# Order of loads, memsets, q and k of chunk 1, quad 0's loads and the last scores in a fused mixer, FFN and attention kernel

## What is computed

```python
x = x + _L0_attn_a_ref(_layernorm(x, axis=-1), ...)   # sigmoid gate, conv of 4 and of 9 taps, linear maps
x = x + _L0_ffn_ref(_layernorm(x, axis=-1), ...)      # relu(h)**2 between two ternary matrices
x = x + _L0_attn_b_ref(_layernorm(x, axis=-1), ...)   # q, k, v; softmax(q k / sqrt(8)) v; out_w
x = x + _L0_ffn_ref(_layernorm(x, axis=-1), ...)
```

## Time and profile before

| | us |
|---|---|
| median of three runs (548.97 to 550.91) | 549.75 |
| the profiled execution's own time | 550.75 |
| its span in the trace | 548.8 |
| TensorE matmuls busy | 508.4 (93%) |
| VectorE busy | 448.9 (82%) |
| ScalarE busy | 355.5 (65%) |
| GpSimd busy | 63.4 (12%) |

### The profile page before, as it was taken

How to read it: one execution, slowest core, us unless ns; L and a number is a source line. 1 busy time by engine, 2 the same in 40 slices (tenths; PEclk the granted TensorE clock), 3 DMA queues, 4 the chain that set the end, 5 groups by cost and what they waited for, 6 DMA issues and landing times.

```text
span 548.8 us, 10459 instructions
## 1 busy us (share of the span) xinstructions
PE 508.4 (93%) x4214; PEld 234.3 (43%) x4214; DVE 448.9 (82%) x666; ACT 355.5 (65%) x680; POOL 63.4 (12%) x89
## 2 busy tenths in 40 slices
PE   1999997997598999999999999999999999999797
PEld 1455455675233333333333333333333333343476
DVE  5799149977698899999999999999999999711853
ACT  2646322433003788888888888888888888887431
POOL 4690002841000000000000000000000000000000
PEclk9999999899655899999999999999999999999999
DMA  8100000023710030201200200200200000000001
GB/s 216 26 3 2 1 1 1 4 81 120 227 37 1 2 79 23 57 2 26 55 3 22 59 3 19 61 2 20 61 2 2 2 2 3 1 2 1 1 20 58
DMA packets 14074, 17.97 MB, mean 33 GB/s; under 512 B 3599, under 2 KB 10174, under 8 KB 13502
## 3 DMA queue, kind: packets, MB, share of 16 engines
q1 hardware_dynamic: 13000, 16.58, 11.1%
q0 software_dynamic: 240, 0.46, 0.4%
q10 hardware_dynamic: 786, 0.27, 0.2%
HBM read 11.70 MB, written 5.24 MB: 31 GB/s over the span
## 4 chain that ended last, share of the span: by engine, by line
PE 81%; DVE 10%; ACT 3%; SPq 2%; issue 1%; DMA 1%; ACTq 1%
PE ps L1235 30%; PE ps L1283 26%; PE ps L1006 7%; PE ps L1016 5%; DVE mx L920 4%; PE ps L1250 4%; PE ps L1027 2%; DVE h L705 2%; PE ps L1052 1%; PE ps L1038 1%; PE ps L1063 1%; DVE x L813 1%; DVE st L682 1%; ACT gate L651 1%; SPq L338 1%
## 5 line engine op out<-in xcount | busy, mean ns | idle before, releaser
L920 DVE TENSOR_REDUCE mx<-ps 128x1 f32<-128x1024 f32 x256 | 311.4, 1224 | 18.7 <-PE ps L1235 16.6
L1235 PE MATMUL ps<-kt,qt 62*128 62x512 f32 x512 | 198.2, 473 | 8.9 <-DVE mx L920 4.6
L1250 PE MATMUL ps<-qt,kt 64*128 64x512 f32 x512 | 188.6, 448 | 1.0 <-ACT gate L651 1.0
L651 ACT ACTIVATE acc<-ps 128x512 f32<-128x512 f32 x256 | 139.2, 597 | 27.4 <-PE ps L1250 22.0
L651 ACT ACTIVATE gate<-ps 128x512 f32<-128x512 f32 x256 | 138.7, 597 | 16.3 <-PE ps L1250 10.4
L1235 PEld LDWEIGHTS ps<-kt,qt 62*128 62x128 f32 x512 | 82.1, 198 | 114.5 <-DVE mx L920 86.0
L1283 PE MATMUL ps<-gate,val 128*32 128x256 f32 x1024 | 82.7, 395 | 3.8 <-ACT gate L651 3.8
L1250 PEld LDWEIGHTS ps<-qt,kt 64*128 64x128 f32 x512 | 77.7, 186 | 11.7 <-ACT gate L651 5.4
L1283 PE MATMUL ps<-acc,val 128*32 128x256 f32 x1024 | 81.6, 391 | 0.4 <-ACT acc L651 0.4
L1283 PEld LDWEIGHTS ps<-gate,val 128*32 128x32 f32 x1024 | 20.2, 108 | 49.3 <-issue 26.8
L1283 PEld LDWEIGHTS ps<-acc,val 128*32 128x32 f32 x1024 | 20.2, 108 | 46.7 <-ACT acc L651 23.4
(11 more groups left out here) (180 smaller groups left out, 389.0 us busy)
## 6 DMA issues: line engine op xcount, KB each, us to landing
kt<-k_scr SPq DMA_DIRECT2D x32, 128.0 KB
qt<-q_scr SPq DMA_DIRECT2D x64, 64.0 KB
x<-in_L_attn_a_x SPq DMA_DIRECT2D x4, 256.0 KB, 5.2
q_scr<-attn SPq DMA_DIRECT2D x4, 256.0 KB, 2.6
k_scr<-attn SPq DMA_DIRECT2D x4, 256.0 KB, 3.1
q_scr<-gate SPq DMA_DIRECT2D x4, 256.0 KB, 2.7
k_scr<-gate SPq DMA_DIRECT2D x4, 256.0 KB, 2.7
qt<-nm_s SPq DMA_DIRECT2D x64, 4.0 KB
```

What stands on the lines that cost most here:

```text
L651: act.activation(pexp[step % NPB][:, j, :], bank(e_bank(slot)), ACT.Exp, scale=SCALE).then_inc(e_read, 1)
L920: dve.tensor_reduce(mx[:, item % 2, at:at + 1], pair(lo), AX.X, ALU.max).then_inc(m_read, 1)
L1235: mm = pe.matmul(bank(m_banks(M_UNIT[u])[keys]), qt[r][rows, half, jj, c * P:(c + 1) * P], kt[r][rows, jj, keys, :], start=True, stop=True)
L1250: pe.matmul(bank(e_bank(slot)), kt[r][rows, jj, s // TC, s % TC * P:(s % TC + 1) * P], qt[r][rows, half, jj, :], start=True, stop=True).th ...
```

## The change

Nothing is computed differently. What moves:

- **Loads.** SP issues x parts 0 and 1, then hb_w, ha_w and fuse_w (512 KB, new semaphore `s_w_fold`), then x parts 2 and 3; taps, the other mixer weights and the FFN's small ones follow, and the two big ternary inputs come last.
- **Roots and folded weights.** ScalarE takes `first_std(0)` as its first work and `first_std(1)` only after the four values of batch 0. TensorE turns hb_w, ha_w and fuse_w right behind in_w, and the vectors (`vec_n`) after the first two `turn_h` and no longer ahead of them.
- **Zeroing.** GpSimd's memsets of `qt`, `kt` and `v4` no longer wait for the mixer's last tokens but for the end of the convolutions (`conv_done`) and for `u_mm`; the row of ones comes from `fu_n`; the bias on x is added between quads of the attention.
- **q and k of chunk 1.** `turn_h`, `qk` and `v` of chunk 1 come ahead of `proj(2)`; VectorE does `qkv_out(0)` and `qkv_out(1)` together; ScalarE copies chunk 2 before its root.
- **Quad 0 in parts.** q of the first query half is loaded as soon as chunk 0 is stored, k after chunk 1, q of the second half last, on a semaphore of its own (`q1_in`) for which only the second item waits.
- **The last 12 steps.** Heads go in the order 2, 0, 3, 1, `pv` is one part of 512 columns, and from the second of these steps banks 4 and 5 join the three banks of the scores.

```diff
+LAST_HEAD = 1
+LATE_HEADS = (2, 0, 3, 1)
+LATE_EBANKS = (4, 5)
+def has_units(hn, s):
+    return HT * (hn + 1) + LEAD + 2 * s < NU
+def heads(hn, s):
+    return HEADS if has_units(hn, s) else LATE_HEADS
...
 def e_bank(slot):
-    return EBANKS[slot % len(EBANKS)]
+    if slot < E_LATE:
+        return EBANKS[slot % len(EBANKS)]
+    at = (slot - E_LATE) % (len(EBANKS) + len(LATE_EBANKS))
+    return EBANKS[(E_LATE + at) % len(EBANKS)] if at < len(EBANKS) else LATE_EBANKS[at - len(EBANKS)]
...
-            for c in range(NCH):
+            def load_x(c):
                 sp.dma_start(x[:, TC * c:TC * c + TC, :], x_src[:, TC * c:TC * c + TC, :]).then_inc(s_x[c], 16)
+            load_x(0)
+            load_x(1)
+            for dst, src in ((hb_n[:, :], hb_w), (ha_n[:, :], ha_w),
+                             (fu_n[:, :, :], fuse_w.rearrange("(k p) c -> p k c", p=P))):
+                sp.dma_start(dst, src).then_inc(s_w_fold, 16)
+            load_x(2)
+            load_x(3)
...
-            for i in range(2):
-                sp.wait_ge(scr_done[i], STORED)
-            load_quad(0)
+            sp.wait_ge(scr_done[0], STORED)
+            load_q(0, 0)
+            sp.wait_ge(scr_done[1], STORED)
+            load_k(0)
+            load_q(0, 1)
...
-            pool.wait_ge(tok_read, TOK_MIX[-1] + 1)
+            pool.wait_ge(setup_mm, 4)
+            pool.memset(ones_home, 1.0).then_inc(consts_ready, 1)
+            pool.wait_ge(conv_done, 2 * B)
+            for r in range(NBUF):
+                pool.memset(qt[r][:, :, :, :].bitcast(F32), 0.0).then_inc(consts_ready, 1)
+                pool.memset(kt[r][:, :, :, :].bitcast(F32), 0.0).then_inc(consts_ready, 1)
+            pool.wait_ge(u_mm, 1)
...
+            first_std(0)
             act.wait_ge(s_norm, 16)
             ev(1, flat(in_T), bank(1), ACT.Identity, scale=norm_col[:, 0:1])
-            first_std(0)
...
-                if c >= 2:
-                    qkv_out(c - 2)
+                if c == 2:
+                    qkv_out(0)
+                    qkv_out(1)
                 take_tokens(TOK_F1, c)
...
+            turn_h(2, TURN_QKV + 1)
             qk(0)
             v(0)
-            turn_h(2, TURN_QKV + 1)
-            proj(2, 0, TOK_F1)
             qk(1)
             v(1)
+            proj(2, 0, TOK_F1)
             proj(3, 0, TOK_F1)
...
+                    if not has_units(hn, s):
+                        for j in LATE_HEADS:
+                            exp_mm(hn, s, j)
+                        pv(step - 1, 0, CH)
+                        continue
```

More of the change, by code:

```diff
@@ L87, in plan @@
                 turned_o[hn // 2 - 1] = next(m)
-            for j in HEADS:
+            for j in heads(hn, s):
                 exps[hn, s, j] = next(e)
@@ L277, in build @@
         qk_in = [sem(f"qk_in{r}") for r in range(NBUF)]
+        q1_in = [sem(f"q1_in{r}") for r in range(NBUF)]
         shift_in, v4_ready = sem("shift_in"), sem("v4_ready")
@@ L304, in _ @@
                 sp.dma_start(dst, src).then_inc(s_w_taps, 16)
-            sp.dma_start(wfc_n[:, :, :], wfc_d.rearrange("(m p) d -> p m d", p=P)).then_inc(s_w_tern, 16)
-            sp.dma_start(wpr_n[:, :], wproj_d).then_inc(s_w_tern, 16)
-            for dst, src in ((pw_n[:, :, :], pw_w.rearrange("(k p) c -> p k c", p=P)), (hb_n[:, :], hb_w),
-                             (ha_n[:, :], ha_w), (fu_n[:, :, :], fuse_w.rearrange("(k p) c -> p k c", p=P)),
-                             (ow_n[:, :], out_w), (bm_n[:, :], Bm_d)):
+            for dst, src in ((ow_n[:, :], out_w), (bm_n[:, :], Bm_d),
+                             (pw_n[:, :, :], pw_w.rearrange("(k p) c -> p k c", p=P))):
                 sp.dma_start(dst, src).then_inc(s_w_mix, 16)
@@ L334, in load_quad, with load_q @@
                         sp.dma_start(dst.rearrange("x j h t -> x (j h t)"), src).then_inc(qk_in[n % NBUF], 16)
-                        for half in range(2):
-                            src = q_scr[i, b, half, rows, :, :].rearrange("d j t -> d (j t)")
-                            dst = qt[n % NBUF][at:at + PARTS * HD, half, :, :].bitcast(F32)
-                            sp.dma_start(dst.rearrange("x j t -> x (j t)"),
-                                         src.unsqueeze(1).broadcast_to([HD, PARTS, RJ * CH])).then_inc(
-                                             qk_in[n % NBUF], 16)
+            def load_q(n, half):
+                b, g = divmod(n, GQ)
+                landed = (qk_in, q1_in)[half][n % NBUF]
+                for a in range(2):
+                    rows = slice((a * GQ + g) * HD, (a * GQ + g + 1) * HD)
+                    for i in range(PARTS):
+                        at = a * HALF + i * PARTS * HD
+                        src = q_scr[i, b, half, rows, :, :].rearrange("d j t -> d (j t)")
+                        dst = qt[n % NBUF][at:at + PARTS * HD, half, :, :].bitcast(F32)
+                        sp.dma_start(dst.rearrange("x j t -> x (j t)"),
+                                     src.unsqueeze(1).broadcast_to([HD, PARTS, RJ * CH])).then_inc(landed, 16)
+            def load_quad(n):
+                load_k(n)
+                load_q(n, 0)
+                load_q(n, 1)
             def load_shift(hn):
@@ L423, in _ @@
             pool.wait_ge(v4_zero, NV)
-            for r in range(NBUF):
-                pool.memset(qt[r][:, :, :, :].bitcast(F32), 0.0).then_inc(consts_ready, 1)
-                pool.memset(kt[r][:, :, :, :].bitcast(F32), 0.0).then_inc(consts_ready, 1)
-            pool.memset(ones_rows, 1.0).then_inc(consts_ready, 1)
             for r in range(NV):
@@ L430, in _, with bias_rows @@
             pool.wait_ge(v4_ones, NV)
-            for c in range(NCH):
+            def bias_rows(c):
                 tiles = slice(TC * c, TC * (c + 1))
@@ L647, in _ @@
                         act.wait_ge(pv_mm, step - NPB + 1)
-                    for at, j in enumerate(HEADS):
+                    for at, j in enumerate(heads(hn, s)):
                         slot = E_EXP[hn, s, j]
@@ L1268, in turn_o, with pv @@
                 mm.then_inc(m_mm, 1)
-            def pv(step, part):
+            def pv(step, lo_q, hi_q):
                 hn, s = divmod(step, BT)
                 n, half = divmod(hn, 2)
-                if part == 0:
-                    pe.wait_ge(e_read, E_EXP[hn, s, HEADS[-1]] + 1)
+                if lo_q == 0:
+                    pe.wait_ge(e_read, E_EXP[hn, s, LAST_HEAD] + 1)
                 first, last = (half, s) == (0, 0), (half, s) == (1, BT - 1)
-                if first and part == 0:
+                if first and lo_q == 0:
                     pe.wait_ge(v4_ready, n + 1)
@@ L1280, in pv @@
                         pe.wait_ge(o_copied, n)
-                lo, cols = VPAD * (1 - half), slice(part * CH // 2, (part + 1) * CH // 2)
+                lo, cols = VPAD * (1 - half), slice(lo_q, hi_q)
                 for j in range(QH):
                     mm = pe.matmul(bank(O_BANK)[VW * j:VW * (j + 1), cols], v4[n % NV][:, s, j, lo:lo + VW],
-                                   pexp[step % NPB][:, j, cols], start=first and part == 0, stop=last and part == 1,
+                                   pexp[step % NPB][:, j, cols], start=first and lo_q == 0, stop=last and hi_q == CH,
                                    tile_position=(0, VW * j))
-                if part:
+                if hi_q == CH:
                     mm.then_inc(pv_mm, 1)
```

125 lines of the change are left out of this document (73 added, 52 removed).

## The result

The changed kernel takes 534.75 us (median of four runs, 534.02 to 536.34), beside 549.92 us for four runs of the kernel before (548.97 to 550.91): a ratio of 0.973, 95% interval 0.970 to 0.976, some 15 us. The prediction was 536.2 with a range of 531.5 to 541. The profiled execution of the changed kernel took 534.02 us with a span of 532.0, so span against span it is 16.8 us shorter; it was the shortest of its four.

The account below looks back on a forecast made before the run. TensorE was taken as the bound most of the time, with five places to gain. Terms of -0.2 + 0.9 + 3.3 + 4.0 + 5.5 = 13.5 us off 550.75 gave 537.2, as a median 536.2, range 531.5 to 541.

Parts of the forecast that it names:

- start: From launch to the first products: x part 2 lands later and takes back other savings, a loss of 0.2 us.
- folded weights: Eight transposes move from TensorE's full stretch at 43.62 into a rest before the first h: gain of 0.9 us.
- zeroing: FFN 1: without memsets beside them four tensor_scalar run faster and TensorE's clock stays at 2.4 GHz: gain of 3.3 us.
- q and k of chunk 1 with quad 0 in parts: Way into attention: first scores wait for the last v at 138.6, not loads at 142.65: gain of 4.0 us.
- last steps: Last 12 attention steps: eleven fall from 2.46 to ScalarE's pace of 1.96 us: gain of 5.5 us.
- the units and first exponentials: At the first scores: the clock was taken to fall to half again, so no gain.
- the ternary part would be stretched to about 14 us: VectorE's ternary weights beside the moved memsets: tensor_scalar held up by them, lasting to about 70.3, costed at nothing.
- rival 2: Last steps: pv and scores hand over too late, step stays near 2.26; gain 2.2 there, 539.5 us; chance 0.15.
- estimate of 4.2: Last steps: the skill's exponential price of 0.52 us gives a step of 2.08 and this smaller gain; the row was preferred.
- rival 3: First scores: the clock stays at 2.4 GHz when the units follow at once; 2.4 us more, 533.8; chance 0.15.
- Rival 5: Last steps: the clock falls and stays low to the end; 559.2 us as a median, at least; chance 0.02.
- Rival 4: FFN 1: the clock falls anyway or gating slips past 77.7; price 1.7 to 2.6 us, 538.3; chance 0.13.

Follow-up runs that it names:

- zero_old: The changed kernel with the zeroing of qt, kt and v4 back behind the mixer's last tokens; 538.31 us.
- folds_late_x_first: folds_late with all four parts of x ahead of the three folded weights on the load queue; 535.82 us.
- seven kernels with the changed start: The changed kernel and six follow-up kernels whose start was not edited; they reach the first transpose of ow_n at 40.47 to 42.16 us.
- folds_late: The changed kernel with the eight transposes of hb_w, ha_w and fuse_w back behind the taps; 538.0 us.
- proj_first: The changed kernel with proj(2) of FFN 1 again ahead of q and k of chunk 1, loads still in parts; 536.52 us.
- quad_whole: The changed kernel with quad 0 loaded whole behind the stores of both chunks; 535.44 us.
- late_3banks: The changed kernel without the two extra banks in the late steps, scores still paired and pv whole; 543.21 us.
- both_old: The changed kernel with the older forms of both proj_first and quad_whole; 537.82 us.
- best: warm_start with projections as single tiles in eight late steps, an early Exp table load, and an earlier second root and sigmoid; 533.38 us.
- warm_start: The changed kernel with nine transposes of the identity ahead of the fold transposes and four behind them; 533.04 us.
- best2: best with the first projection whole in its old place and the second ahead of the last pv; 532.15 us.
- warm_units_256: The changed kernel with a whole-array product of 256 columns behind each of the first 24 units; 559.98 us.

## Why the prediction was right, point by point

The forecast of 536.2 lies 1.5 above the median of 534.75, inside its range. The six terms against what was measured in the profiled executions: start -0.2 against 3.15; folded weights 0.9 against 0.93; zeroing 3.3 against 3.05; q and k of chunk 1 with quad 0 in parts 4.0 against 3.39 (the 6.44 between A and B less zero_old's 3.05); last steps 5.5 against 5.38; the units and first exponentials 0 against 0.90. Sum 16.8, predicted 13.5.

**Start.** This is the term that was mis-sized most. The step "512 KB put ahead of part 2 move it by 3.6 to 10.9" failed: part 2 was there at 9.22, the norm began at 10.48 and not 12.3, and the first product at 14.00 and not 15.6. By folds_late_x_first the mechanism was right: part 2 holds the norm, and without the weights ahead of it the norm comes 2.1 us sooner. I had scaled loads that queue behind one another, by the spacing of the earlier trace rows; the loads overlapped (hb_w landed at 6.11, 0.23 behind x part 1) and part 2 landed at 9.19 instead of 7.32, a shift of 1.9. The second half of the 3.15 wasn't in the sum at all. TensorE's first products take 1.06 to 1.22 us each before they take 0.59, and how many do so differs between executions: sixteen took 9.97 in the kernel before, 8.05 to 9.27 in the seven kernels with the changed start. The prediction took the products' own time as fixed. The changed kernel's profile was the luckiest of these; by their mean of 41.47 to A the start and the folds together gain 3.1 and not 4.1, and the whole 15.8, nearer to the medians' 15.2. How many executions of the kernel before are as slow as its profile isn't known; one was looked at.

The Trainium skill, "TensorE: Matmul & The Clock Gate" (Part 1), says that the number of slow products at a kernel's start varies from run to run. The traces agree: of the same sixteen, two to five took over 0.9 us in the seven kernels with this start, 8.05 to 9.27 us in all.

**Folded weights.** As computed; 0.93 is read directly in folds_late.

**Zeroing.** Right in both halves, the wait and the clock (3.3 taken, 3.05 measured); zero_old brings back both the 2.74 and the 5.13. The forecast that the ternary part would be stretched to about 14 us was wrong in its place in time: GpSimd was still busy with `xr` until 56.91 and the memsets began at 57.37, after the ternary part had ended (54.89 + 0.94). Nor did the convolutions end later: 47.1, since none of their operations was held up (below). Neither moved the sum, as both were costed at nothing.

**q, k and quad 0.** The forecast that no load would be waited for held. The share of the order of products was too large (1.0 in the sum: 138.6 against 139.6): that order is worth 0.72 by proj_first, and the parts as such nothing by quad_whole. The rest, some 2.7 us, is the wait for the landing of the earlier trace rows, which is gone in every variant that has q's second half on its own semaphore and last on the queue; that this is the cause was read and not run. The last `v` was added at 131.87, a full 7.75 earlier than before, of which 7.1 came from upstream.

**Last steps.** The main part held: eleven steps of 1.96 at ScalarE's pace. Each projection adds 0.79 to a step (0.84 taken). Two small things differ, and that 5.38 lies so near 5.5 is in part luck. TensorE nowhere waits for `load_shift`, for which I had taken 0.5 off. In its place the last `pv` waits 0.90 for ScalarE where it waited 0.37 before, a loss of 0.53, and the first late step, still on three banks, takes 2.66 and not 2.46. late_3banks shows that the hand-over latencies, not TensorE's work, decide here, as rival 2 had it, though with three banks only. Four paired scores and a `pv` do take TensorE 1.66 where the banks are free (479.96 to 481.62). The prediction's estimate of 4.2 by the Trainium skill, "ScalarE: Activation LUTs" (section "What ACT_TABLE_LOAD costs"), was too low; the row was the better price.

**Clock.** It fell at the first scores, so rival 3 is out as worded; whether a high clock there would pay stays open. The fall came some 3 us behind the first units instead of ahead of them, and the rise 7.3 us behind the first score of an exponential (162.14 to some 169.5) instead of 8.3 (173.2 to some 181.5). B to C became 0.52 shorter, and the kernels of the table whose clock fell later behind the first scores have the shorter B to C: 30.04 with the fall 1.4 behind (zero_old), 29.77 with 3.8 (quad_whole). The other 0.38 of the 0.90 lies within the spread of C to D. Rival 5 needed a low clock in the late steps: the windows show none there. Rival 4 is out by the rows of FFN 1.

## What to carry to other kernels

When a long rotation ends and another engine sets the pace, a better order for TensorE can lose without spare banks (2.5 us here) and gain with them (5.4): count whether the next step's inputs can be ready while the paced engine still works through this one, and give the rotation the banks that fell idle. Before you cost a wait for a group of loads, ask which of them the first consumer needs; by my reading of both_old, a semaphore for the rest, with its loads last on the queue, did more than moving the work. Compare profiles between marks inside the program, since one stretch (here the start) can vary by 1.7 us in identical code and another (C to D) by 0.9, while three repeat within 0.1.

## What the runs showed of the hardware

- The rows say a granted clock of 1.00 at the start, but the first products take up to twice the later ones' time, until the first clock record of the trace. Short work is slow there too: the four transposes of fuse_w take 1.06 us at 9.30 in the changed kernel, 0.60 at 44.11 in the kernel before, and 0.60 at 9.11 in best, whose first record stands at 7.73. In the changed kernel from 14 to 23 us (duration min/median/max):

```profile
L1073 PE MATMUL ps<-hT,in_T x16: 592/592/1221, 14.0 to 21.5; 128*128 128x512 f32 x16
```

  Read the durations there, not the clock row. Thirteen transposes more in front made all of them fast in warm_start and best (7.13 and 7.21 us) and not in best2 (8.60); their first records stand at 12.26, 7.73 and 17.66.
- TensorE can be busy all the time and stay at 1.2 GHz (24.00 of 24.00 us at 0.50 in warm_units_256), while the same program in other runs had a mean of 0.996.
- VectorE and GpSimd held each other up, and which of them lost differed with the very same operations. In both kernels GpSimd began its sixteen `tensor_scalar` on `xr` ahead of the convolutions (18.11 against 22.70, 22.38 against 23.79). In the kernel before they took 11.27 us, and one convolution step took 3.37. In the changed kernel they took 26.68, one of them alone 12.32 (from 23.68 on) while VectorE went through 20 operations without a gap, and no convolution step took over 0.77. GpSimd and VectorE of the kernel before, then of the changed one:

```profile
18.11 11.27 POOL L412 TENSOR_SCALAR xr<-x,xr_c,small 128x128 f32<-128x128 f32 x16 [5.51 <-DVE small L765]
...
L412 POOL TENSOR_SCALAR xr<-x,xr_c,small x16: 439/441/1396, 18.1 to 28.0; 128x128 f32<-128x128 f32 x16
L789 DVE SCALAR_TENSOR_TENSOR acc<-val,ksym,acc x32: 739/764/3367, 23.6 to 49.8; 128x512 f32<-128x512 f32 x32
```

```profile
22.38 26.68 POOL L453 TENSOR_SCALAR xr<-x,xr_c,small 128x128 f32<-128x128 f32 x16 [10.12 <-DVE small L821]
...
L453 POOL TENSOR_SCALAR xr<-x,xr_c,small x16: 438/1378/12316, 22.4 to 48.6; 128x128 f32<-128x128 f32 x16
L845 DVE SCALAR_TENSOR_TENSOR acc<-val,ksym,acc x32: 736/742/772, 24.7 to 46.4; 128x512 f32<-128x512 f32 x32
```

  The Trainium skill, "SBUF — State Buffer" (section "Who interferes with whom"), says that issue order, not the shape of an operation, decides who is blocked. The traces agree that the same shapes can be blocked either way; that the order decides they don't show, as GpSimd's operations began first in both.
- In several of these executions (zero_old, quad_whole, proj_first, warm_start among them) the clock was at 1.2 GHz for some 3 us near the last turn of the output (mean 0.57 from 495 to 499 in quad_whole). E to the end is 39.64 to 39.71 with it and without: the chain that ended last goes through VectorE there (493.0 to 503.0 in the changed kernel).
